# A decoder block on one core: split gate and up products, a reordered attention setup, and finer waits on gathered tiles

## What is computed

```python
x = layernorm(x + attention(x))          # 16 heads of 32, causal softmax
x = layernorm(x + chosen(x, ctx))        # token id picks 1 of 4 experts; Wg = Wu = Wd = ctx[e], 512 x 512
# routed feed-forward, 8 experts of width F = 352, top 2 of the softmax, plus a shared expert of width 1408
expert_out = vmap(lambda wg, wu, wd: silu(x @ wg) * (x @ wu) @ wd)(Wg, Wu, Wd)
moe_out    = einsum('te,eth->th', C, expert_out)      # C: the two routing weights of a token, else 0
shared     = sigmoid(x @ Wsg) * (silu(x @ Sg) * (x @ Su) @ Sd)
x = layernorm(x + moe_out + shared)
```

## Time and profile before

| | |
|---|---|
| median of three executions | 1361.4 us |
| the profiled execution | 1363.77 us |
| its span, first to last instruction | 1362.0 us |
| mean granted TensorE clock | 0.945 |
| busy: TensorE / VectorE / ScalarE / GpSimd | 1226.3 / 629.3 / 436.4 / 234.9 us |
| share of the chain that ended last: TensorE | 54% |
| DMA traffic | 169.65 MB, mean 125 GB/s |

### The profile page before, as it was taken

How to read it: one execution, slowest core, us unless ns; L and a number is a source line. 1 busy time by engine, 2 the same in 40 slices (tenths; PEclk the granted TensorE clock), 3 DMA queues, 4 the chain that set the end, 5 groups by cost and what they waited for, 6 DMA issues and landing times.

```text
span 1362.0 us, 19276 instructions
## 1 busy us (share of the span) xinstructions
PE 1226.3 (90%) x6068; PEld 924.4 (68%) x6068; DVE 629.3 (46%) x1420; ACT 436.4 (32%) x682; POOL 234.9 (17%) x355
## 2 busy tenths in 40 slices
PE   4778999899998659996799999999999999899995
PEld 3556676676676447884578888677777777678884
DVE  3735456456457235664547743211111211576754
ACT  3034434333434402221433333233332322233331
POOL 0012313412413310001300640000000000333200
PEclk9788899899799779998899999999999999999998
DMA  7144443643422411222523664244444441566440
GB/s 214 39 138 149 125 149 115 196 139 108 122 67 76 133 62 56 84 78 80 184 70 93 232 233 135 75 129 139 127 141 127 136 132 51 159 186 192 148 131 31
DMA packets 129270, 169.65 MB, mean 125 GB/s; under 512 B 17552, under 2 KB 70800, under 8 KB 129168
## 3 DMA queue, kind: packets, MB, share of 16 engines
q1 hardware_dynamic: 115264, 136.38, 32.7%
q0 software_dynamic: 8496, 28.32, 6.2%
q10 hardware_dynamic: 5408, 3.68, 1.1%
HBM read 95.98 MB, written 47.19 MB: 105 GB/s over the span
## 4 chain that ended last, share of the span: by engine, by line
PE 54%; DVE 4%; POOL 2%; DMA 1%; issue 1%; ACT 1%; ACTq 0%; POOLq 0%; DVEq 0%
PE routed_ps L1312 14%; PE routed_ps L1366 14%; PE routed_ps L775 7%; PE chosen_psG L775 4%; PE chosen_psY L775 4%; PE routed_ps L1331 2%; PE routed_ps L1333 2%; PE routed_ps L1332 2%; POOL routed_rows_io L1256 1%; PE routed_ps L1353 1%; PE routed_ps L1377 1%; PE chosen_psX L856 1%; DVE routed_s_lo L1627 1%; PE chosen_psH L875 1%; PE routed_ps L1277 1%
## 5 line engine op out<-in xcount | busy, mean ns | idle before, releaser
L1366 PE MATMUL routed_ps<-routed_wgu,routed_xT_f 128*128 x624 | 191.7, 460 | 1.6 <-ACT routed_xT_f L1470 1.1
L423 PE MATMUL psT<-store 128*128 128x512 f32 x576 | 161.8, 429 | 6.1 <-DVE store L639 4.3
L1366 PEld LDWEIGHTS routed_ps<-routed_wgu,routed_xT_f 128*128 128x128 f32 x624 | 115.4, 190 | 61.0 <-issue 2.9
L709 DVE CUSTOM_DVE_ANT_0 psS<-psS,attn_mask 128x512 f32<-128x512 f32 (+3 forms) x256 | 119.1, 511 | 45.9 <-PE psS L489 45.4
L423 PEld LDWEIGHTS psT<-store 128*128 128x128 f32 x576 | 117.2, 211 | 33.4 <-DVE store L639 3.1
L595 ACT ACTIVATE acc<-psE 128x512 f32<-128x512 f32 x160 | 93.7, 599 | 132.2 <-PE psE L510 130.7
L368 POOL TENSOR_SCALAR_AFFINE_SELECT acc<-acc 128x256 f32<-128x256 f32 (+1 forms) x160 | 58.2, 369 | 327.0 <-ACT acc L595 325.9
L1256 POOL DMA_INDIRECT routed_rows_io<-sorted_y,routed_pos x32 | 37.6, 1174 | 440.9 <-DMA sorted_y<-routed_rows_io 366.3
L1312 PE MATMUL routed_ps<-routed_later,routed_s_hi 128*128 128x512 f32 x352 | 89.1, 396 | 4.7 <-issue 2.9
L489 PE MATMUL psS<-attn_kS,attn_qS 96*128 96x512 f32 (+3 forms) x256 | 67.2, 344 | 28.6 <-DVE attn_rowmax L709 21.3
L775 PE MATMUL routed_ps<-routed_first 128*128 x351 | 91.3, 404 | 0.0
(11 more groups left out here) (240 smaller groups left out, 1984.2 us busy)
## 6 DMA issues: line engine op xcount, KB each, us to landing
sorted_x<-attn_zero SPq DMA_DIRECT2D x19, 768.0 KB, 4.1
routed_sraw<-in_L_ffn_Sg_dram SPq DMA_DIRECT2D x44, 256.0 KB, 3.1
routed_sraw<-in_L_ffn_Su_dram SPq DMA_DIRECT2D x44, 256.0 KB, 3.5
routed_sraw<-in_L_ffn_Sd_dram SPq DMA_DIRECT2D x44, 256.0 KB, 3.9
routed_rows_io<-sorted_x SPq DMA_DIRECT2D x39, 256.0 KB, 2.7
sorted_y<-routed_rows_io SPq DMA_DIRECT2D x39, 256.0 KB, 2.1
attn_qS<-attn_ch_hi SPq DMA_DIRECT2D x128, 64.0 KB, 2.0
attn_kS<-attn_ch_hi SPq DMA_DIRECT2D x112, 64.0 KB, 2.0
```

Source lines behind the costliest of these rows:

```text
L423: last = pe.matmul(out, lhs[a](k), rhs[c](k), start=(s[-1] == 0 and k == 0), stop=(s[-1] == 2 and k == KC - 1))
L709: last = dve.tensor_tensor_reduce(scores, scores, mask[:, (3 - t) * P:T], 1.0, BELOW_ALL, ALU.add, ALU.max, rowmax[:, g % 2, t, i:i + 1])
L1366: last = pe.matmul(out, xT_f[:, s % 2, k, :], wgu[:, bass.ds(b, 1), at:at + F].rearrange("p a n -> p (a n)"), start=(k == 0), stop=(k == K ...
```

## The change

The gate and up products of a routed tile become three-part products: 24 of 352 columns in place of 8 full float32 ones. For this ScalarE and VectorE split the turned tile and, on a change of expert, the gate and up weights; the weights land in one raw buffer and are split into two slots, one of which lies over the shared expert's split weights. In the attention phase, the setup is put in another order, the broadcast loads go from ScalarE's to SyncE's queue, the one-hot copies go to GpSimd, TensorE begins with 24 transposes of the identity, clearing of the scratch tensors runs at up to two pieces per step, and blocks of ctx have four buffers (two of them the tiles `zero` and `bv`). The gathered tiles 0 to 3 have a semaphore each. The diff, cut to its core; an @@ line names the function and the engine. VectorE has the same new steps as ScalarE in the routed phase, with the subtractions that give x_lo, gu_lo and wd_lo. split_first(0) and split_first(1), the first expert's gate and up weights, are split in steps 18 and 19 of the shared expert:

```diff
--- before.py
+++ after.py
@@ attention_steps @@
-    steps += product("V", 0, 0) + [("CNT",), ("RT2", 0)] + product("V", 0, 1) + [("RT2", 1)] + product("V", 0, 2) + [("RT2", 2)]
+    steps += product("V", 0, 0) + [("CNT",), ("RT2", 0)] + product("V", 0, 1) + product("V", 0, 2)
...
-            fill += [("CW", n) for n in range(7)]
+            fill += [("CW", n) for n in range(5)]
...
-            fill += [("CW", n) for n in range(7, 14)]
+            fill += [("CW", n) for n in range(5, 9)]
...
+            if m in (4, 7) and s == 0:
+                one += [("RT2", 1 + m // 7)]
...
-    steps += [("PV", NG - 1, j) for j in range(QT)] + [("CW", 14), ("NH", 0), ("CW", 15), ("NH", 1)]
+    steps += [("PV", NG - 1, j) for j in range(QT)] + [("NH", 0), ("CW", 9), ("NH", 1)]
...
+    steps += [("CW", n) for n in range(10, 16)]
@@ attention_phase @@
+        cw_rows = [x_in[:, 0, :], x_in[:, 1, :], zero[:], bv[:]]
+        def cw_landed(n):
+            return (x_ready[n % 4], 16 * (2 * (B - 1) + 2 + n // 4)) if n % 4 < 2 else (cw_in[n % 4 - 2], 16 * (n // 4 + 1))
@@ attention_phase, SyncE @@
+            sp.dma_start(bv[:], b_attn[2 * C:3 * C].partition_broadcast(P)).then_inc(bias_in, 16)
+            sp.dma_start(bp[:], b_proj.partition_broadcast(P)).then_inc(bias_in, 16)
             sp.wait_ge(w_lo_done, 2)
...
             def load_cw(n):
-                was = ("XT", B - 1, n + 2) if n < 2 else ("CW", n - 2)
-                sp.wait_ge(sh_full[bank_of[was]], use_of[was] + 1)
-                sp.dma_start(x_in[:, n % 2, :], ctx_w[n // KC, (n % KC) * P:(n % KC + 1) * P, :]).then_inc(x_ready[n % 2], 16)
+                if n == 2:
+                    sp.wait_ge(clear1_done, 16 * n_clear1)
+                    sp.wait_ge(clear2_done, 16 * n_clear2)
+                elif n == 3:
+                    was = ("V", B - 1, QT - 1)
+                    sp.wait_ge(sh_free[bank_of[was]], use_of[was] + 1)
+                else:
+                    was = ("XT", B - 1, n + 2) if n < 2 else ("CW", n - 4)
+                    sp.wait_ge(sh_full[bank_of[was]], use_of[was] + 1)
+                sp.dma_start(cw_rows[n % 4], ctx_w[n // KC, (n % KC) * P:(n % KC + 1) * P, :]).then_inc(cw_landed(n)[0], 16)
...
-                    if g >= 2 and pieces:
-                        clear()
-                if s[0] == "CW" and s[1] + 2 < E * KC:
-                    load_cw(s[1] + 2)
+                    if g >= 2:
+                        for _ in range(min(2, len(pieces))):
+                            clear()
+                if s[0] == "CW" and s[1] + 4 < E * KC:
+                    load_cw(s[1] + 4)
@@ attention_phase, GpSimd, ahead of its steps @@
+            pool.wait_ge(consts_ready, 8)
+            for n, part in enumerate(kS):
+                if n:
+                    pool.wait_ge(onehot_done, n)
+                pool.tensor_copy(part[AUX:AUX + 4, :, :],
+                                 onehot[AUX:AUX + 4, :].unsqueeze(2).broadcast_to([4, 4, T])).then_inc(onehot_done, 1)
+            pool.wait_ge(onehot_done, 3)
@@ attention_phase, TensorE @@
             pe.wait_ge(ident_done, 1)
+            for _ in range(24):
+                pe.transpose(psO[:, 0:P], ident[:], ident[:])
@@ attention_phase, ScalarE @@
-            act.dma_start(bv[:], b_attn[2 * C:3 * C].partition_broadcast(P)).then_inc(bias_in, 16)
-            act.dma_start(bp[:], b_proj.partition_broadcast(P)).then_inc(bias_in, 16)
@@ attention_phase, VectorE: in ("V", 0, i), and no longer in ("K", 0, 2) @@
+                    if s == ("V", 0, 2, 2):
                         dve.wait_ge(w_hi_done, 5)
                         dve.tensor_tensor(wp_lo[:], p_f[:, 0:4, :], wp_hi[:].bitcast(F32), ALU.subtract).then_inc(w_lo_done, 1)
-                    if s[1] == 0 and s[2] < 3:
-                        dve.tensor_copy(kS[s[2]][AUX:AUX + 4, :, :],
-                                        onehot[AUX:AUX + 4, :].unsqueeze(2).broadcast_to([4, 4, T])).then_inc(onehot_done, 1)
@@ routed_phase @@
+        held = sb("held", [P, AT + 4 * GW], F32R)
-        wgu = sb("wgu", [P, 3, 2 * WG], F32)
-        xT_f = sb("xT_f", [P, 2, KC, P], F32)
+        gu_raw = sb("gu_raw", [P, GW], F32)
+        x_hi, x_lo = (part[:].rearrange("p b (k n) -> p b k n", k=KC) for part in (h_hi, h_lo))
@@ routed_phase, SyncE @@
-                    for s in range(3):
-                        load_up(s)
+                    load_up(0)
                     load_down(0)
...
             load_down(1)
+            for s in (1, 2, 3):
+                load_up(s)
             for s in range(NS):
...
-                if s + 3 < NS:
-                    sp.wait_ge(up_full, s + 1)
-                    load_up(s + 3)
                 if s + 2 < NS:
                     load_down(s + 2)
+                if s + 4 < NS:
+                    load_up(s + 4)
@@ routed_phase, GpSimd @@
                 pool.indirect_dma_start(out=acc[:, t, :], out_offset=None, in_=chosen_y,
-                                        in_offset=bass.IndirectOffsetOnAxis(ap=chosen_pos[:, t:t + 1], axis=0)).then_inc(x2_in[t // QT], 16)
+                                        in_offset=bass.IndirectOffsetOnAxis(ap=chosen_pos[:, t:t + 1], axis=0)).then_inc(x2_in[t if t < QT else QT - 1 + t // QT], 16)
@@ routed_phase, TensorE @@
-                if t % QT == 0:
-                    pe.wait_ge(x2_in[t // QT], 16 * QT)
+                if t < QT:
+                    pe.wait_ge(x2_in[t], 16)
+                elif t % QT == 0:
+                    pe.wait_ge(x2_in[QT - 1 + t // QT], 16 * QT)
...
-            def up(s):
-                b = entry(pe, t_slot3, s, 2)
-                pe.wait_ge(x_ready, s + 1)
+            def up(s, b):
+                pe.wait_ge(x_low, s + 1)
...
-                    for k in range(KC):
-                        at = m * WG + k * F
-                        last = pe.matmul(out, xT_f[:, s % 2, k, :], wgu[:, bass.ds(b, 1), at:at + F].rearrange("p a n -> p (a n)"),
-                                         start=(k == 0), stop=(k == KC - 1))
+                    w = [lambda k, part=part: part[:, bass.ds(b, 1), m * WG + k * F:m * WG + (k + 1) * F].rearrange("p a n -> p (a n)")
+                         for part in (gu_hi, gu_lo)]
+                    last = products(pe, out, x, w, KC)
...
+                was = slot
+                if s + 1 < NS:
+                    slot = entry(pe, t_slot, s + 1, 1)
                 turn_h(s)
@@ routed_phase, ScalarE @@
             def turn_x(s):
-                act.wait_ge(wgu_in, ONE + version * 32 + 32)
-                act.copy(xT_f[:, s % 2], t_x[s % 2].rearrange("p (k n) -> p k n", k=KC)).then_inc(x_ready, 1)
+                act.copy(x_hi[:, s % 2], t_x[s % 2].rearrange("p (k n) -> p k n", k=KC)).then_inc(x_high, 1)
+            def split_gu(changed, version, b):
+                with act.If(changed > 0):
+                    for m in range(2):
+                        part = slice(m * WG, (m + 1) * WG)
+                        act.wait_ge(gu_in[m], ONE + version * 16 + 16)
+                        act.copy(gu_hi[:, bass.ds(b, 1), part].rearrange("p a n -> p (a n)"), gu_raw[:, part]).then_inc(gu_high, 1)
...
-            split_w(0)
             turn_x(0)
+            split_first(2)
+            plans = [plan(1)]
+            act.wait_ge(s_down, PART)
+            split_gu(*plans[0])
             for s in range(NS):
...
                 if s + 1 < NS:
                     turn_x(s + 1)
+                else:
+                    split_up(PART)
+                if s + 2 < NS:
+                    plans.append(plan(s + 2))
+                    split_gu(*plans[1])
                 if s:
                     copy_y(s - 1)
...
                 if s + 1 < NS:
-                    split_w(s + 1)
+                    split_w(*plans.pop(0))
+            split_down(PART)
```

More of the change, by code:

```diff
@@ L1213, in _ @@
         def _(pool):
-            for s in (wgu_in, wd_low, wdraw_in):
+            for s in (*gu_in, gu_low, wd_low, wdraw_in):
                 pool.sem_inc(s, ONE)
@@ L1235, in _ @@
             pool.memset(wdraw[rows[-1]:P, WD - C:WD], 0.0).then_inc(filled, 2)
-            for q in range(NQ):
-                pool.wait_ge(x2_in[q], 16 * QT)
+            for n, landed in enumerate(x2_in):
+                pool.wait_ge(landed, 16 if n < QT else 16 * QT)
             for t in range(NT):
@@ L1354, in turn_x @@
                 last.then_inc(x_turned, 1)
-            def up(s):
-                b = entry(pe, t_slot3, s, 2)
-                pe.wait_ge(x_ready, s + 1)
+            def up(s, b):
+                pe.wait_ge(x_low, s + 1)
                 if s >= 2:
                     pe.wait_ge(h_done, s - 1)
+                x = [lambda k, part=part: part[:, s % 2, k, :] for part in (x_hi, x_lo)]
                 for m, out in ((0, t_gate[s % 2]), (1, t_up[s % 2])):
@@ L1458, in shared_step @@
             def shared_step(n):
-                if n + 1 < len(steps):
```

(3 more changed lines are left out.)

160 lines of the change are left out of this document (103 added, 57 removed).

## The result

The kernel after takes 1307.4 us (median of four executions, 1304.9 to 1309.7), the kernel before 1361.9 beside it. The ratio is 0.9608, 95% interval 0.9576 to 0.9640: 3.9% faster. One of the four executions of the kernel before took 3101.05 us and is left out of the ratio. The forecast was 1306 us, with a range of 1292 to 1330. The profiled execution took 1309.7 us, its span is 1308.0.

The account below looks back on a forecast made before the run. TensorE's work was taken to bound the shared half and routed loop, waits the setup and attention's end. Loop -27.6, entry -1.1, exit +0.6, head -2.7, setup -14.5, attention's end -9.5: -54.8, from 1361.4 to 1306 us, range 1292 to 1330.

Parts of the forecast that it names:

- Rival (b): Setup and attention's end give only half, since another wait comes next and the clock stays low: +12 us, 1318; chance 0.15.
- (a): Routed loop: narrow products keep part of a wide one's price, 0.185 us each: 1328 us in all; chance 0.12.
- (c): Routed loop: the register-addressed weight load sets TensorE's pace; break-even at 0.221 us per product, 1393 us at 0.255; chance 0.04.
- (d): Changes of expert: the single raw buffer lets weights come late, 4 us each: +22 us, 1328; chance 0.05.
- (e): Routed loop: the clock falls, at 0.9 the 269 us loop grows by 28 us, 1334 in all; chance 0.04.
- the sentence on GpSimd's copies: Attention setup: by the skill's rule GpSimd's copies could hold up VectorE's first remainders by 2.4 us, leaving 12 instead of 14.5.
- +2.5 for RT2 in group 0: Attention group 0: RT2 parts 2 and 3 now lie where row maxima wait behind them, costing 2.5 us (0 to 4).
- The -6 for group 15: End of attention: with four buffers and nine instead of fourteen blocks before the last PV, ScalarE bounds group 15: -6 us.
- Group 14 loses two blocks: -1.5: End of attention: group 14 has two fewer blocks of chosen weights to turn, saving 1.5 us.
- NH and PV of group 15: End of attention: NH no longer waits behind CW 14, -1.8 us; PV(15) and PR, partly at the lower clock, -1.
- The six late blocks: Very end of attention: six chosen-weight remainders on VectorE behind LN2 delay the phase's end by 0.8 us.
- the second four gathers then take back up to 1 us: Head of routed phase: gathers issued 5 us behind the first reduce the 3.1 us gain; term taken as -2.7 us.

Follow-up runs that it names:

- e10: Kernel of e5 run again beside the kernel after on one chip: 1316.5 us, ratio to before 0.9507.
- e4: Kernel after, with the remainder of h on VectorE moved between the gate and up halves of the next expert's subtraction: 1307.4 us, ratio to before 0.9603.
- e6: Kernel after plus 80 identity transposes before TensorE's wait for the first gathered tile, and 10 behind turns 1 and 3: 1331.0 us, ratio to before 0.9615.
- e5: Kernel of e4 with the down weights' split also moved behind silu, h and the x passes of its own iteration: ratio to before 0.9451, on another chip.
- e9: Kernel after, unchanged, run again beside e10 on one chip: 1327.1 us, ratio to before 0.9579.
- e8: Kernel after with two buffers instead of four for the rows of the chosen weights: ratio to before 0.9599.
- e1: Kernel before with only the routed phase's part of the change, still one semaphore for the first four gathers: ratio to before 0.9802.
- e3: Kernel before with only a semaphore for each of the first four gathers: ratio to before 0.9990.
- e2: Kernel before with only the attention phase of the kernel after: ratio to before 0.9814.

## Why the prediction held

| term | predicted | measured |
|---|---|---|
| loop with entry and exit (first `turn_x` to step 22) | -28.1 | -27.3 |
| setup and groups 0 to 12 | -14.5 | -14.0 |
| end of attention | -9.5 | -8.2 |
| chosen phase | 0 | -2.7 |
| head and first shared half | -2.7 | -1.1 |
| second shared half | 0 | -0.7 |
| sum | -54.8 | -54.0 |

The mechanisms of the loop and the setup were right in the main. That the sum is right within 1 us is partly luck: the four terms named in the forecast gave 50.6 of their 54.8 us, and 3.4 us came from stages that it had put at 0, 2.7 of them not the change's doing.

**The loop.** The price per product was taken as 0.162 and is 0.165 us; a change was to cost 0.8 and costs 0.84 on its own tile. With the tile behind it, it costs 1.2: the tiles of after exceed 6.74 us by 8.5 us in all, where 5.6 were forecast, and e10 wins 8.6 by removing them. The forecast had counted only the wait of `down`. That wait's mechanism, the remainder of h behind two subtractions, was named and e4 confirmed it by moving it. Rival (b) falls with the table: setup and end gave 22.2 of 24 us. Rivals (a), (c), (d) and (e) fall: 0.165 is below 0.185 and 0.221, no wait at a change is for gate or up weights, the clock stays at 1.00. (At 0.9 of the clock the 269 us of (e) would have grown by 30 us, not by its 28.) Under "The mechanism" on the page "TensorE: Matmul & The Clock Gate" the Trainium skill lets a weight load overlap only a product of other row groups; products of full height that repeat in 0.122 and 0.165 us don't agree with it. The first paragraph of that section also names a background weight buffer as a second case, with which these rows would agree; no row tells which it is.

**Setup.** The first row maximum came at 36.5, not 34: Q started as forecast, at 14.06, but VectorE's w_proj remainder, forecast to begin at 31, began at 34.30, behind ScalarE's copy. The gain there was 15.8 instead of 17 us, and 14.0 is left at group 13. That Q started on time was luck of the execution: of eleven traces with the new order only after and e6 have it at 14.06 and 13.33, the others at 15.6 to 15.8. The step that failed there is the sentence on GpSimd's copies, which the sum put at nothing and whose price stood beside it as up to 2.4 us: two subtractions that take 2.36 us before take 5.4 to 5.8 in these nine traces (last section). The rest of the term, +2.5 for RT2 in group 0, wasn't isolated. VectorE does 2.8 us more in group 0 (13.4 for 10.6 us). From the first mask of group 0 to that of group 2 it takes 57.8 us in after and 53.7 to 57.8 in eight other traces of the new order, but 51.9 and 51.7 in e5 and e9, against 51.6 to 52.7 with the old order. So most executions lose 2 to 6 us there and some lose nothing; RT2's passes and the doubled clears are both candidates, and no run parts them.

**End of attention.** From the first mask of group 13 to the chosen phase's first transpose 96.3 us became 88.1, and 84.9 to 85.0 in e4, e5, e9 and e10. By parts, in after: from the first mask of group 13 to that of group 15, +4.3 us; from there to group 15's last mask, -5.8; to the projection's first product, -5.4; to the chosen phase, -1.3. The -6 for group 15 is borne out in size, but the buffers aren't its cause, since e8 with two buffers has it too; the fewer blocks are left as its cause. The step that failed is "Group 14 loses two blocks: -1.5": TensorE, which has fewer blocks to turn there, is idle 2.25 us ahead of group 14's PV (0.95 before) and does most of its 64 products at the lower clock. The same products before, then in after:

```profile
446.50:451.00 4.50, 4.44 (x64) 1.94 (x64) 0.69 (x1) 0.00 (x0) 0.01 (x1) 1.00 0.30 96
```

```profile
433.90:441.30 7.40, 7.33 (x64) 2.40 (x64) 0.26 (x1) 0.00 (x0) 0.02 (x1) 0.59 0.09 37
```

That is 2.9 us of the 4.3; no run puts the blocks back to show that they are the cause. What came in its place: NH and PV of group 15, put at 2.8 us together with the projection, gave 5.4 up to the projection's first product, since that PV ran at the upper clock (4.45 us, 6.47 before). The six late blocks were put at 0.8 us; they do hold the first load, which comes 4.2 us behind the last scatter's issue, 3.8 before.

**Head.** The mechanism was right and the term too large. The step that failed is "the second four gathers then take back up to 1 us"; what took back 2.1 us is the clock, which I had not counted there.

**The chosen phase** is unchanged in code. Its 2.7 us are the execution's, not the change's: from first transpose to first gather it takes 138.1 us in the trace of before, but 135.7 and 135.3 in e1 and e3, whose code up to there is the same; it takes 137.9 in e2, whose attention is that of after.

## What to carry over

Read the price of a matmul as columns times a constant only where two widths of the trace agree, then multiply by the count; here that alone gave half the gain to within 1 us. When a wait is taken away, list the next two users of the engine that was late, since the stall moved by one tile until both splits had left the critical place. An earlier start that spreads small pieces of TensorE work can cost the clock what it wins in waiting; so can taking filler work out of a stretch in which TensorE waits. An engine that stands idle isn't free for every instruction: the copies moved to GpSimd held VectorE up. And one trace can show the lucky order of two engines, so look at several.

## What the runs showed of the hardware

- Short bursts didn't keep TensorE's upper clock reliably. In after, behind the 24 transposes and a pause of 1.03 us, 8 transposes took 1.41 us, and after a further pause of 1.27 us the next 8 took 1.97; the mean granted clock from 7 to 14 us is 0.70. In e6, whose start has the same code, they took 1.39 and, after a pause of 1.19 us, 1.25.
- Two-input VectorE passes and GpSimd's one-hot copies, which read and write the same memory, held each other up for whole instructions. A copy alone takes 1.89 us, a subtraction 1.23. In after the first subtraction begins 0.01 us ahead of the second copy, which then takes 2.97; from there each instruction ends some 1.1 (subtraction) or 1.8 us (copy) behind the end of the other engine's:

```profile
5.78 1.23 DVE L651 TENSOR_TENSOR store<-acc,store 128x1024 fp32r<-128x1024 f32 x1 [5.78 <-ACT store L568]
5.79 2.97 POOL L380 CAST attn_kS<-attn_onehot 4x2048 fp32r<-4x2048 f32 x1
8.10 1.74 DVE L651 TENSOR_TENSOR store<-acc,store 128x1024 fp32r<-128x1024 f32 x1 [1.09 <-ACT store L568]
8.83 2.77 POOL L380 CAST attn_kS<-attn_onehot 4x2048 fp32r<-4x2048 f32 x1
```

In e9, and alike in eight more traces, the second copy is first, and both subtractions wait for a copy to end:

```profile
5.79 1.89 POOL L380 CAST attn_kS<-attn_onehot 4x2048 fp32r<-4x2048 f32 x1
6.03 2.73 DVE L651 TENSOR_TENSOR store<-acc,store 128x1024 fp32r<-128x1024 f32 x1 [6.03 <-ACT store L568]
7.75 2.77 POOL L380 CAST attn_kS<-attn_onehot 4x2048 fp32r<-4x2048 f32 x1
8.68 2.90 DVE L651 TENSOR_TENSOR store<-acc,store 128x1024 fp32r<-128x1024 f32 x1
```

The Trainium skill, "SBUF — State Buffer", section "SBUF: two separate sides", describes a pair that excludes each other for whole instructions; the traces agree. The cost is 0.5 us in after and 3.2 in e9 (5.56 for 2.36 us), where the prediction had worked out up to 2.4 from copies of 1.22 us.

- Chips differ by 20 us for the same kernel. In e9 the stretch from first gather to first `turn_x` takes 231.7 us instead of 212.3, more than the 13.9 us between the two spans. While the routed scatters run, TensorE is idle again and again between single products, with no releaser in the profile; the same 25 us, counted from the first gather, in e9 and in after:

```profile
755.00:780.00 25.00, 15.83 (x48) 10.37 (x47) 6.50 (x8) 5.46 (x8) 12.93 (x14) 0.73 0.50 183
```

```profile
761.00:786.00 25.00, 25.00 (x112) 20.70 (x111) 9.91 (x12) 8.39 (x13) 10.54 (x11) 1.00 0.67 235
```

What TensorE lacks there stays open, and no run tests it. Two versions are therefore to be compared on one chip.
